# A fused attention and mixture-of-experts kernel: in each quad TensorE runs the small step after the values instead of before them

## What is computed

```python
h = tok_ref(x, W, b, pos_embed)                      # 16 x 1024 tokens x 64
h = h + attn_ref(layernorm(h), ...)                  # 8 heads of 8 dims, per-column bias
h = h + moe_ref(layernorm(h), ...)                   # 8 experts, top 2
# attention of one batch:
scores = einsum('bihd,bjhd->bhij', q, k) / sqrt(8) + col_bias
attn = softmax(scores, axis=-1)                      # 8 x 1024 x 1024 per batch
out = einsum('bhij,bjhd->bihd', attn, v) @ Wo + bo
```

## Time and profile before

| | |
|---|---|
| time, median of 3 runs | 1233.62 us (1233.39 to 1233.87) |
| the profiled execution: its time | 1236.53 us |
| its span, first to last instruction | 1234.4 us |
| TensorE matmul (PE) busy | 1131.4 us, 92% |
| ScalarE (ACT) busy | 1034.6 us, 84% |
| VectorE (DVE) busy | 733.6 us, 59% |

### The profile page before, as it was taken

The page is one execution under the profiler, slowest core; times in us unless marked ns, Lnnn a source line. Parts: engine busy times, 40 slices in busy tenths (PEclk is TensorE's granted clock), DMA queues, the critical chain, the costliest instruction groups (busy, mean ns, idle before and its releaser), DMA issues. The chain is left out here.

```text
span 1234.4 us, 23590 instructions
## 1 busy us (share of the span) xinstructions
PE 1131.4 (92%) x8738; PEld 343.7 (28%) x8738; DVE 733.6 (59%) x1956; ACT 1034.6 (84%) x1124; POOL 118.6 (10%) x128
## 2 busy tenths in 40 slices
PE   2269999999999999999999999999999999899998
PEld 2022222222222222222222222222222222243332
DVE  8634365656565656565656575757575641567654
ACT  0059999999999999999999999999999999945553
POOL 4303010101010101010100000000010100000000
PEclk9999999999999999999999999999999999999999
DMA  1133131323131313131323122222222130022231
GB/s 39 53 79 82 37 82 47 81 49 81 49 80 50 80 50 79 50 80 50 79 51 79 50 74 56 66 59 67 61 68 60 54 84 10 14 64 69 65 85 48
DMA packets 61672, 75.96 MB, mean 62 GB/s; under 512 B 25988, under 2 KB 31108, under 8 KB 61532
## 3 DMA queue, kind: packets, MB, share of 16 engines
q1 hardware_dynamic: 59452, 73.78, 23.6%
q10 hardware_dynamic: 1600, 0.27, 0.1%
q0 software_dynamic: 480, 0.06, 0.1%
HBM read 37.47 MB, written 36.49 MB: 60 GB/s over the span
## 5 line engine op out<-in xcount | busy, mean ns | idle before, releaser
L1134 ACT ACTIVATE probs<-psum 128x1024 f32<-128x1024 f32 x1024 | 951.2, 1105 | 46.1 <-PE psum L1327 45.4
L1343 PE MATMUL psum<-probs,VA 128*32 128x512 f32 x4096 | 545.6, 605 | 8.2 <-DVE oT L1202 7.4
L1327 PE MATMUL psum<-QA,KA 54*128 54x512 bf16 x2048 | 349.6, 386 | 34.1 <-ACTq L1153 10.4
L1327 PEld LDWEIGHTS psum<-QA,KA 54*128 54x128 bf16 x2048 | 81.5, 93 | 536.0 <-ACT probs L1134 493.4
L1343 PEld LDWEIGHTS psum<-probs,VA 128*32 128x32 f32 x4096 | 82.6, 108 | 139.0 <-issue 104.9
L1202 DVE STREAM_TRANSPOSE oT<-psum 128x512 f32<-128x512 f32 x64 | 45.8, 715 | 122.9 <-PE psum L1343 122.4
L1169 ACT ACTIVATE probs<-psum,b 128x1024 f32<-128x1024 f32 x64 | 67.8, 1110 | 54.2 <-PE psum L1396 54.2
L1274 DVE TENSOR_TENSOR probs<-probs,psum 128x1024 f32<-128x1024 f32 x64 | 78.1, 1221 | 51.4 <-PE psum L1406 31.6
L1134 ACT ACT_TABLE_LOAD x1 | 1.3, 1283 | 72.5 <-issue 72.5
L1396 PE MATMUL psum<-m_x,w 64*128 64x512 f32 x256 | 60.5, 591 | 1.5 <-ACT probs L1169 1.5
L1420 PE MATMUL psum<-probs,w 128*64 128x512 f32 x256 | 60.9, 598 | 0.0
(11 more groups left out here) (185 smaller groups left out, 934.6 us busy)
## 6 DMA issues: line engine op xcount, KB each, us to landing
QA<-q_parts_d SPq DMA_DIRECT2D x64, 192.0 KB
KA<-k_parts_d SPq DMA_DIRECT2D x64, 192.0 KB
q_parts_d<-qk_parts SPq DMA_DIRECT2D x32, 192.0 KB, 2.5
k_parts_d<-qk_parts SPq DMA_DIRECT2D x32, 192.0 KB, 2.7
xT<-in_xT SPq DMA_DIRECT2D x16, 256.0 KB, 3.4
q_parts_d<-qk_parts SPq DMA_DIRECT2D x32, 128.0 KB, 2.7
k_parts_d<-qk_parts SPq DMA_DIRECT2D x32, 128.0 KB, 2.6
x_d<-x2T SPq DMA_DIRECT2D x16, 256.0 KB, 2.0
```

The lines of the kernel that those rows point to most:

```text
L1134: nc.scalar.activation(probs[:, k % PROB_BUFS, :], score_buf(buf_of(k)), ACT.Exp).then_inc(exped, 1)
L1327: last = pe.matmul(score_buf(buf_of(k))[:, (g % 2) * BANK:(g % 2 + 1) * BANK], KA[rows_of(h, SCORE_ROWS), h // 2, jt * P:(jt + 1) * P], QA ...
L1343: last = pe.matmul(o_acc[32 * g:32 * g + 32, :], VA[:, jt, h, :], probs[:, k % PROB_BUFS, (g % 2) * BANK:(g % 2 + 1) * BANK], start=(jt == ...
```

## The change

On TensorE, the loop over `steps_of(q, ...)` is moved behind the call of `values`, in all quads. Nothing else is changed; the other engines' lists stay as they are, row for row.

```diff
                         scores(b, q)
-                        for step in steps_of(q, not last, not first):
-                            i = order.index(step)
-                            aux_step(step, b + 1 if step in PREP else b - 1, aux_base(b) + i + 1, aux_base(b) + i)
                         if q >= LAG:
                             values(b, q - LAG)
                         elif not first:
                             values(b - 1, QUADS + q - LAG)
+                        for step in steps_of(q, not last, not first):
+                            i = order.index(step)
+                            aux_step(step, b + 1 if step in PREP else b - 1, aux_base(b) + i + 1, aux_base(b) + i)
```

## The result

The changed kernel takes 1323.34 us (median of 4 runs, 1319.92 to 1325.35) against 1233.7; the ratio is 1.0724, 95% interval 1.0699 to 1.0749. The forecast was 1285, its range 1262 to 1300. The sign was right, the size was not: 89.6 us were lost instead of 51.

What follows compares the result with a forecast made beforehand. ScalarE and TensorE were taken as jointly at their limit. Waits of 3.49 us a batch, less in the first and last, total 51.4: 1236.5 becomes 1287.9, less 2.9 for the median, forecast 1285 us, range 1262 to 1300.

Steps and rivals of the forecast that it cites:

- What bounds the kernel: ScalarE and TensorE both at their limit; near ScalarE's idle spells each microsecond TensorE loses reaches the end.
- The four waits: Values wait for VectorE's transpose in quads 2, 10, 18, 26: 0.23, 1.29, 1.56, 0.41 us; 3.49 a batch.
- Reordering at nothing: Between one quad's scores and the next, the work is the same in both orders, so reordering itself costs nothing.
- the clock rival: New waits slow TensorE's clock for about three quads behind quad 18: 3.4 us a batch, 50 in all; 4%.
- The range: 8 in 10, 1262 to 1300 us, from the likeliest case's 1272 towards the bare transposes, and up for ScalarE's losses.
- the 1335: Forecast time in us if the new waits slowed TensorE's clock behind quad 18; chance 4%.

Runs made afterwards that it cites:

- The run that filled quad 18: The changed kernel with six unused bf16 matmuls into the free aux bank between scores and values of quad 18: 1289.25 us, ratio 1.0424.

## Why the prediction was wrong

- **What bounds the kernel** was right. Each wait put on TensorE next to ScalarE's idle spells came out as idle time of ScalarE.
- **The four waits** were right in place and cause. By ScalarE's idle time they cost 0.29, 1.15, 1.60 and 0.27 us a batch in quads 2, 10, 18 and 26, for 0.23, 1.29, 1.56 and 0.41 forecast; 3.31 for 3.49. The run that filled quad 18 shows the total without the clock, 52.6 us for 51.4. That it comes so near is partly luck: batches 1 to 14 grew by 47.8 us for 48.9, the first and the last together by 5.1 for 2.5. The errors in quads 10 and 26 are one: the transpose starts 0.08 us before the drain's row ends (569.62 against 568.89 + 0.81), where 0.04 behind was taken.
- **Reordering at nothing** was right: no drain was late for a step with the whole order changed. In the runs that changed only some quads it was wrong: TensorE's quad grew by 0.44 us (`v` behind `qk1`) and by 0.40 (`flag` behind `out_proj`) where a step in the old order came in the quad after one in the new.
- **The step that failed is the rejection of the clock rival**, "after a wait of 1.50 in the expert part eight matmuls took 2.13 us, or 0.27 each, no sign of the lower level. 4%." One wait that did no harm was taken as proof for all, and the term was put at nothing. It measured 37 us. The run with the transposes first has twelve waits of 1.5 to 1.8 us in quad 18 that did no harm and three that did, in one execution. The earlier trace rows was one such sample, and in other surroundings. The rival's price, 3.4 us a batch or 50 in all, was near: 2.7 and 37.
- **The Trainium skill's rule** (TensorE: Matmul & The Clock Gate, "What's actually happening"), that the rate is halved when the array was idle and given back when it is busy, described what happened better than my reading of the row. The traces agree on the halving: at 0.50 the values take 1.94 us for 1.07. By the rule alone each of the new waits is a candidate; the traces show that most are harmless (none of the 15 of 1.08 us in quad 10 had a drop behind it, 2 of 30 of 1.68 us), so the rule does not say which wait brings the clock down.
- **The range** rested on four durations that the trace gave well. It should have held a share for the one effect that the new waits could have on what lies around them: it reached to 1300 and left the 1335 out. Its own working ends at 1293; what lies between that and 1300 has no term.

## What to carry to other kernels

Before work is moved out from between a producer's last write and the wait for the bank's release, look at what it covers, and at what is queued ahead of the releasing instruction on the other engine: here one loop moved behind four lines uncovered a transpose and the run of work ahead of it. A new wait on TensorE of 1.5 us and more is to be priced twice, once by its length and once by what the matmuls behind it cost at half rate, and one harmless wait in the trace is little evidence against the second. Where such a wait can't be avoided, useless matmuls into a free bank can keep the clock, as they did here. Cutting the long steps up over several quads won 1% over the kernel before; moving them lost 7.2%.

## What the runs showed of the hardware

- A wait of 1.5 to 1.76 us in quad 18 stands in 15 batches of five kernels. In the profiled executions the clock fell behind it in 14 of them after the change, in 3 with the transposes first, in 15 with these and six matmuls more in quad 3, in 8 with `out_proj` a quad later, and in 3 with one matmul of 0.22 us more in each of two quads ahead. In the changed kernel successive drops lay 68.27 us apart over eight batches whose own lengths were 68.33 to 68.82.
- The first batch, without `out_proj`, has a wait of 1.53 to 1.54 us in quad 18 in nine of the kernels. The clock fell behind it in three of them and not in six.
- A stretch at 0.50 in attention lasted 3.41, 6.83 or 10.24 us: 6.83 or 10.24 in every case where `out_proj`, fp32 matmuls with 64 columns, came right behind the wait, and 3.41 in all others (the 8 with `out_proj` a quad later, the first batch, which has none, and the two behind quad 10).
